# Two triangle layers on one core: quadrants kept in SBUF, LayerNorm roots by Newton's method on VectorE

## The reference, cut to what matters

```
layer 0: z = LN(x);  a = (z@W_ap + b) * sigmoid(z@W_ag + b) * mask;  b likewise
         out[i,j,c] = sum_k a[i,k,c] * b[k,j,c];   x = x + out@W_z + b_z
layer 1: x' = LN(x);  left, right = sigmoid(x'@w1) * (x'@w2)
         p[s,k,e] = sum_r left[s,r,e] * right[k,r,e];  p = LN(p)
         x = x + (p@out_w) * sigmoid(x'@gate)
```

## Time and profile before

| | us |
|---|---|
| median of 3 runs (992.37 to 997.83) | 995.39 |
| the profiled execution's own time | 993.22 |
| its span | 991.6 |
| steps 11 to 47 (VectorE starts of their statistics) | 46.9 to 172.4 |
| contraction 0, first to last matmul | 226.0 to 268.3 |

### The profile page before, as it was taken

How to read it: one execution, slowest core, us unless ns; L and a number is a source line. 1 busy time by engine, 2 the same in 40 slices (tenths; PEclk the granted TensorE clock), 3 DMA queues, 4 the chain that set the end, 5 groups by cost and what they waited for, 6 DMA issues and landing times.

```text
span 991.6 us, 26391 instructions
## 1 busy us (share of the span) xinstructions
PE 817.9 (82%) x9820; PEld 786.3 (79%) x9820; DVE 763.9 (77%) x1851; ACT 635.0 (64%) x866; POOL 590.0 (59%) x410
## 2 busy tenths in 40 slices
PE   4654444567999899989899999999999999999865
PEld 3553344467899799989899999898999898989754
DVE  6899999987589958995388888708980897069896
ACT  5698888765667536753266777547763776257664
POOL 7699999987256504660376444405661667068887
PEclk9789999798999999999899999999999999999999
DMA  4455489988789718969665768857982797876675
GB/s 139 117 161 150 131 275 297 342 286 299 256 274 316 226 33 270 307 205 282 235 194 156 241 214 297 325 193 215 296 279 66 216 306 225 291 253 226 212 233 191
DMA packets 173397, 228.75 MB, mean 231 GB/s; under 512 B 11224, under 2 KB 109784, under 8 KB 171224
## 3 DMA queue, kind: packets, MB, share of 16 engines
q1 hardware_dynamic: 172408, 226.96, 71.7%
q10 hardware_dynamic: 864, 0.12, 0.1%
HBM read 134.76 MB, written 92.27 MB: 229 GB/s over the span
## 4 chain that ended last, share of the span: by engine, by line
PE 43%; DVE 20%; DMA 15%; issue 11%; POOL 4%; ACT 3%; SPq 3%; DVEq 0%; POOLq 0%; ACTq 0%
PE bank L1117 18%; PE ps_w L1151 6%; DVE stats L944 6%; PE bank L1097 6%; DMA xin<-in_x_dram 6%; PE bank L1098 5%; DVE split L988 3%; PE ps_t L1136 3%; DMA xt<-xt 3%; DVE xc L981 2%; DMA xin<-x 2%; PE ps_x L1162 2%; DVE var L951 2%; DVE xc L973 2%; DMA chunk<-xcol 2%
## 5 line engine op out<-in xcount | busy, mean ns | idle before, releaser
L660 POOL TENSOR_TENSOR rstd<-var,minus_half 128x8 f32<-128x8 f32 x192 | 343.8, 1791 | 321.4 <-DVE var L951 321.4
L1117 PE MATMUL bank<-rhs,lhs 128*128 128x128 f32 x1536 | 227.6, 281 | 13.5 <-DVE lhs L924 7.5
L1117 PEld LDWEIGHTS bank<-rhs,lhs 128*128 128x128 f32 x1536 | 200.2, 196 | 16.4 <-DVE lhs L924 8.2
L718 ACT ACTIVATE sig<-bank 128x512 f32<-128x512 f32 x256 | 152.0, 602 | 63.5 <-PE bank L1098 61.1
L745 ACT ACTIVATE xt<-ps_x 128x1024 bf16<-128x1024 bf16 x128 | 130.9, 1022 | 60.6 <-PE ps_x L1162 47.1
L1162 PE MATMUL ps_x<-ident_b,split 128*128 128x128 bf16 x1024 | 83.3, 227 | 95.8 <-DVE split L988 95.3
L1162 PEld LDWEIGHTS ps_x<-ident_b,split 128*128 128x128 bf16 x1024 | 67.1, 102 | 107.3 <-DVE split L988 106.0
L981 DVE TENSOR_TENSOR xc<-xc,rstd 128x504 f32<-128x504 f32 (+1 forms) x192 | 137.9, 718 | 16.1 <-POOL xc L674 13.9
L1097 PE MATMUL bank<-w_rhs,chunk 128*128 128x128 bf16 x1024 | 136.9, 228 | 6.5 <-DVE rhs L916 2.7
L1098 PE MATMUL bank<-w_rhs,chunk 128*128 128x128 bf16 x1024 | 136.0, 227 | 0.0
L1097 PE MATMUL bank<-w_lhs,chunk 128*128 128x128 bf16 x928 | 125.8, 227 | 9.4 <-DVE lhs L916 4.4
(11 more groups left out here) (114 smaller groups left out, 1592.3 us busy)
## 6 DMA issues: line engine op xcount, KB each, us to landing
chunk<-xt SPq DMA_DIRECT2D x90, 512.0 KB, 4.5
xt<-xt SPq DMA_DIRECT2D x80, 512.0 KB, 5.4
xin<-in_x_dram SPq DMA_DIRECT2D x128, 256.0 KB, 4.7
x<-xin SPq DMA_DIRECT2D x64, 256.0 KB, 5.1
xin<-x SPq DMA_DIRECT2D x64, 256.0 KB, 4.9
out_dram<-xin SPq DMA_DIRECT2D x64, 256.0 KB, 4.6
spill<-lhs SPq DMA_DIRECT2D x8, 1024.0 KB, 5.4
chunk<-xcol SPq DMA_DIRECT2D x16, 512.0 KB, 5.6
```

The lines of the kernel that those rows point to most:

```text
L660: g.tensor_tensor(rstd[:, m % 2], var[:, m % 2], minus_half[:, :], ALU.pow).then_inc(rooted, 1)
L718: a.activation(sig[:, s], v[:, 0:C, :], ACT.Sigmoid).then_inc(gated, 1)
L1117: last = mm(bank[:, n], operand_of(q // 4, "lhs", kh)[:, c, :], operand["rhs"][:, kh, c, :], start=kh == 0, stop=kh == HALVES - 1)
```

## The change

- **Roots.** For z steps `variance` and `root` go. VectorE computes the root for a pair of steps (128 × 16 values) in ten small operations, numbered 0 to 9: add eps and scale; an integer operation on the bits that gives a first guess; a step of third order; a Newton step. Each waits on the semaphore of the one before. `root_in_gap()` issues one of them, and is called between the larger operations: between the `bn_stats`, behind `make`, `low`, `normalise`, `mask_unit`. Operation 0 follows the statistics of the odd step at once; 8 and 9 follow those of the next even step together. `stats` has four buffers. Steps 64 and on keep the root on GpSimd.
- **Where operands lie.** From pair 6 (step 12) the intermediate values and the root lie in a bank of PSUM (`newton_p`, in `ps_w`), `guess` and `square` in SBUF; from step 12 the normalised tile of even steps is written to PSUM (`normed_p`, in `ps_t`). Before that all are in SBUF.
- **GpSimd** centres all steps below 128, without waiting for `normalise` of the step before, and takes `low` of odd z steps. Its order in a tick is low, mask, centre. Masks are one a tick from 22 to 69; unit u of contraction 0 waits for its own mask only.
- **Residents.** Columns of quadrant 0 go to the free half of `lhs`, those of quadrant 2 into the memory of `quad`; chunks 16 to 31 (rows of quadrants 0 and 2) are projected from there with a stride. Their 16 loads go, and so do `xt_out` and `store_xt` of those quadrants (32 and 16 issues). Quadrant 2's columns are stored in 8 DMAs of 512 KB in place of 16.
- **Schedule.** All z stages from `norm` on are one tick later. Four "last z" ticks in place of six; the second half takes steps 52 to 55. The spills of `lhs` are spread over contraction 0. `loads` and `loads_diag` are issued in ticks 1 and 3.

```diff
...
-DIRECT = CHUNKS
+DIRECT = 2 * CHUNKS
...
-Z_LAGS = dict(load=-2, stats=0, variance=0, root=0, centre=1, norm=1, high=1, low=2, turn_x=2, xt=3,
-              col=3, store=4, project=3, gates=4, make=5)
+Z_LAGS = dict(load=-2, stats=0, centre=1, norm=2, high=2, low=3, turn_x=3, xt=4,
+              col=4, store=5, project=4, gates=5, make=6)
...
-LATE_Z_LAGS = dict(Z_LAGS, turn_x=3, xt=4, col=4, store=5)
+LATE_Z_LAGS = dict(Z_LAGS, turn_x=4, xt=5, col=5, store=6)
...
-    for m in range(3 * STEPS, Z_LATE - 2):
+    for m in range(3 * STEPS, Z_HALF):
         tick("last z", m)
+    late = dict(zip((1, 3, 4, 6), range(Z_HALF, Z_LATE)))
     for i in range(8):
-        tick("second half", {2: Z_LATE - 2, 5: Z_LATE - 1}.get(i), [48 + 2 * i, 49 + 2 * i], spill=(0, 0, i // 2 - 1) if i in (3, 5, 7) else None)
+        tick("second half", late.get(i), [48 + 2 * i, 49 + 2 * i], spill={6: (0, 0, 0)}.get(i))
     contraction(0, dict(zip((0, 1, 2, 3, 5, 6, 8, 9), range(Z_LATE, 4 * STEPS))),
-                {0: (0, 0, 3), 3: (0, 1, 0), 7: (0, 1, 1), 11: (0, 1, 2), 15: (0, 1, 3)})
+                {2: (0, 0, 1), 4: (0, 1, 0), 6: (0, 0, 2), 8: (0, 1, 1), 10: (0, 0, 3), 12: (0, 1, 2), 15: (0, 1, 3)})
...
-    if MASK_FIRST <= t < MASK_TWO:
-        return [t - MASK_FIRST]
-    if MASK_TWO <= t < MASK_TWO + C // 8:
-        return [2 * C // 4 + 2 * (t - MASK_TWO), 2 * C // 4 + 2 * (t - MASK_TWO) + 1]
-    return []
+    return range(max(0, t - MASK_FIRST), min(POOL_MASKS, t - MASK_FIRST + 1))
...
+def by_rows(m):
+    return step(m)[0] == "x" or step(m)[1] == 1
...
+    if n < DIRECT + 2:
+        return max(stored, TICK_OF[("store", "step", Z_LATE - 1)])
...
-    return m < Z_EARLY or Z_LATE <= m < P_BASE
+    return m < P_BASE
...
+def low_on_pool(m):
+    return m < X_BASE and m % 2 == 1
...
+            return newton_s if 2 * pair < OTHERS_AT + 5 else newton_p
...
+        normed_p = ps_t[:, :, :].rearrange("p n (a c) -> p (n a) c", c=C)
+        def normed_of(m):
+            if OTHERS_AT + 5 <= m < X_BASE and not low_on_pool(m):
+                return normed_p
+            return xc[:, m % 2]
+        def root_of(m):
+            if m < X_BASE:
+                return newton_of(m // 2)[:, 2 + m // 2 % 2, m % 2]
+            return rstd[:, m % 2]
...
+        resident = {0: operand["lhs"][:, 1].rearrange("p c j -> p (c j)").bitcast(BF16),
+                    2: scratch.bitcast(BF16)}
         sig_staged = [sig[:, n].rearrange("p c t -> p (c t)").bitcast(BF16) for n in range(2)]
         SIG_STAGED = Z_LATE
         def col_buffer(m):
-            if m < 2 * STEPS:
+            q, c0 = m // STEPS, step(m)[3]
+            if q in resident:
+                return resident[q][:, P * c0:P * (c0 + COLS)]
+            if m < SIG_STAGED:
                 return chunk[:, (m // 2) % 2, P * COLS * (m % 2):P * COLS * (m % 2 + 1)]
-            if m < SIG_STAGED:
-                return staged[m % 4]
             return sig_staged[m % 2]
...
+            def store_resident(m):
+                _, rh, _, c0 = step(m)
+                sp.wait_ge(col_done, after(m))
+                sp.dma_start(xcol_dram[rh, :, c0 - COLS:c0 + COLS, :],
+                             resident[2][:, P * (c0 - COLS):P * (c0 + COLS)].rearrange("p (j r) -> p j r", r=P)
+                             ).then_inc(resident_stored, 16)
...
+                if t == 1:
+                    for dst, src in loads:
+                        sp.dma_start(dst, src).then_inc(loaded, 16)
...
+                    if m % 2 and by_rows(m):
                         store_xt(m)
-                    if 2 * STEPS <= m < X_BASE:
+                    if m % 2 and m // STEPS == 2:
+                        store_resident(m)
+                    if m // STEPS == 3:
                         store_cols(m)
...
-                pool.wait_ge(normed, after(m - 1))
...
+                    pool.wait_ge(*low_by(m - 2))
...
+            def low(m):
+                h = m % 2
+                pool.wait_ge(high_done, after(m))
+                g.tensor_tensor(split[:, h, :, 1, 1:], xc[:, h, :, 1:], split[:, h, :, 0, 1:],
+                                ALU.subtract).then_inc(low_p, 1)
...
+                for m in due("low", t):
+                    if low_on_pool(m):
+                        low(m)
+                for n in pool_masks_at(t):
+                    mask_operand(n)
...
+                    if by_rows(m):
+                        xt_out(m)
...
-                dve.wait_ge(*centred_by(m - 2))
+                dve.wait_ge(*centred_by(m - 4))
+                if m - 4 < X_BASE:
+                    dve.wait_ge(rooted_z, after(m // 2 - 2))
...
                 for c in range(0, COLS, 2):
+                    if c:
+                        root_in_gap()
...
+            def root(pair, n):
+                count = 9 * pair
+                minus_var, term = (newton_of(pair)[:, i] for i in range(2))
+                result = newton_of(pair)[:, 2 + pair % 2]
+                if n == 0:
+                    dve.wait_ge(rooted_z, after(pair - 1))
+                    dve.wait_ge(stats_done, after(2 * pair + 1))
+                    v.tensor_scalar(minus_var, stats[:, 2 * (pair % 2):2 * (pair % 2) + 2, :, 2],
+                                    C * EPS, NEWTON, ALU.add, ALU.mult).then_inc(newton, 1)
+                if n == 1:
+                    dve.wait_ge(newton, count + 1)
+                    v.tensor_scalar(guess[:, :, :].bitcast(I32), minus_var.bitcast(I32), -0.5, GUESS, ALU.mult, ALU.add
+                                    ).then_inc(newton, 1)
+                if n in (2, 7):
+                    dve.wait_ge(newton, count + n)
+                    v.tensor_tensor(term, minus_var, guess[:, :, :], ALU.mult).then_inc(newton, 1)
+                if n == 3:
+                    dve.wait_ge(newton, count + 3)
+                    v.tensor_tensor(square[:, :, :], term, guess[:, :, :], ALU.mult).then_inc(newton, 1)
+                if n == 4:
+                    dve.wait_ge(newton, count + 4)
+                    v.tensor_tensor(term, term, guess[:, :, :], ALU.mult).then_inc(newton, 1)
+                if n == 5:
+                    dve.wait_ge(newton, count + 5)
+                    v.scalar_tensor_tensor(term, term, -1.25 / NEWTON, square[:, :, :], ALU.add, ALU.mult
+                                           ).then_inc(newton, 1)
+                if n == 6:
+                    dve.wait_ge(newton, count + 6)
+                    v.scalar_tensor_tensor(guess[:, :, :], term, 1.875, guess[:, :, :], ALU.add, ALU.mult
+                                           ).then_inc(newton, 1)
+                if n == 8:
+                    dve.wait_ge(newton, count + 8)
+                    v.scalar_tensor_tensor(term, term, -0.5 / NEWTON, guess[:, :, :], ALU.mult, ALU.mult
+                                           ).then_inc(newton, 1)
+                if n == 9:
+                    dve.wait_ge(newton, count + 9)
+                    dve.wait_ge(normed, after(2 * pair - 3))
+                    v.scalar_tensor_tensor(result, term, 1.5, guess[:, :, :], ALU.add, ALU.mult
+                                           ).then_inc(rooted_z, 1)
+            def root_in_gap():
+                if unfinished:
+                    pair, n = unfinished.pop()
+                    root(pair, n)
+                    if n < 9:
+                        unfinished.append((pair, n + 1))
...
-                v.tensor_tensor(xc[:, h, :, lo:], xc[:, h, :, lo:],
-                                rstd[:, h].unsqueeze(2).broadcast_to([P, COLS, C - lo]),
+                dve.wait_ge(*((rooted, after(m - X_BASE)) if m >= X_BASE else (rooted_z, after(m // 2))))
+                v.tensor_tensor(normed_of(m)[:, :, lo:], xc[:, h, :, lo:],
+                                root_of(m).unsqueeze(2).broadcast_to([P, COLS, C - lo]),
...
+                begun_earlier = [pair for pair, n in unfinished]
+                root_in_gap()
                 for h in halves[:-1]:
                     make(h)
+                    root_in_gap()
                 for m in due("stats", t):
                     statistics(m)
+                    while unfinished:
+                        root_in_gap()
+                    if m < X_BASE and m % 2:
+                        unfinished.append((m // 2, 0))
+                        root_in_gap()
                 for h in halves[-1:]:
                     make(h)
+                    root_in_gap()
                 unit = unit_at(t)
                 if unit and unit[0] in VECTOR_MASKS:
                     mask_unit(*unit)
...
+                for m in due("low", t, "z"):
+                    if not low_on_pool(m):
+                        low(m)
+                        root_in_gap()
+                for m in due("norm", t, "z"):
+                    while unfinished and unfinished[0][0] == m // 2:
+                        root_in_gap()
+                    normalise(m)
+                    root_in_gap()
...
```

(13 more changed lines are left out.)

183 lines of the change are left out of this document (98 added, 85 removed).

## The result

The kernel after takes 1022.1 us (median of four runs, 1017.6 to 1024.8); the kernel before took 996.6 beside it (992.4 to 998.5). The experiments ran in later batches, on different chips, and the kernel before took 993.0 to 996.5 beside them. A difference between two batches is therefore good to some 4 us; the stages of the profiled executions are the finer measure. The ratio is 1.0258, 95% interval 1.0207 to 1.0308. The forecast was 965 (949 to 987): the sign is wrong, and the time is 57 us off.

A forecast was written before the change was run, and what follows sets the result against it. VectorE, with GpSimd close, was taken to bound most of the first 172 us, then DMA, and PE from 226 us. The terms −3 − 3.4 − 9.6 − 15.6 + 1 = −30.6 took 995.4 to 965 us (949 to 987).

The forecast's parts named there:

- Residents: Step 48 to contraction 0: chunk loads and xt stores go, VectorE's gate waits vanish; 53.6 us becomes 38, 15.6 off.
- Start-up: Up to step 11: weight loads move behind later x loads, so step 11 starts 3 us earlier; ends no gain and 3.8.
- the lock: VectorE operations with two SBUF inputs and GpSimd operations exclude each other for a whole instruction; not expected with a PSUM operand.
- Steps 11 to 21: Before the masks start: a step falls from 3.21 to 2.9 us, 3.4 us saved over 11 steps.
- Steps 22 to 47: With masks on GpSimd: a step falls from 3.47 to 3.1 us, 9.6 us saved over 26 steps.
- Second half: Step 48 to the first contraction matmul: four ticks at 3.1 and eight of two chunks at 3.2 each, 15.6 us off.
- Contraction 0: From 226 us: roots leave, GpSimd has a mask in each of ten ticks; 44 us, +1; ends 36 and 52.
- Behind it: After contraction 0: hardly any work changed, spills only delay x loads; no gain or loss in the sum.
- The small operations do not overlap: Rival on the root's operations: each costs 0.22 us, 1.1 a step, VectorE 3.5; 987 us, chance 0.14.
- milder form: Errata rule of fixed cycles per VectorE operation: 0.87 us a step, VectorE 3.25, some 8 us above the forecast.
- The lock holds the small operations: Rival, steps 0 to 51: a PSUM operand does not spare them, 2.25 us a step; +86, about 1080, chance 0.07.
- GpSimd gives it back: Rival: GpSimd's low halves take 1.53 us and contraction 0 takes 52; 12 more, 977 us, chance 0.12.

The follow-up runs named there:

- e15_pitch260: Kernel after with each row of the two resident quadrants beginning 260 bytes behind the last in place of 256, small tiles moved to make room; 976.4 us, ratio 0.9823.
- e7_halves: Kernel after with each resident quadrant stored as two blocks of 64 rows, rows read at 128 bytes, columns loaded as two halves; 979.6 us, ratio 0.9874.
- e5_step260B: Kernel after with chunks 16 to 31 read at a step of 260 bytes, 125 of 128 elements of each vector (wrong vectors); 1033.0 us in one run.
- e6_small_ops_sbuf: Kernel after with chunks 16 to 31 read contiguously (wrong vectors) and all operands of the root's small operations in SBUF; 1077.0 us in one run.

## Why the prediction was wrong

**The step that failed** is "Residents". It removed the loads of chunks 16 to 31 and kept their projections at their old price; that these would now read their stationary operand at 256 bytes in place of 32 stands in the diff and in no term of the sum. The kernel before could have warned: its trace has the same loads at two steps. Contiguous ones took 98 ns (85 to 130 us); the row chunks', at 32 bytes, 149 (142 to 180 us, kernel before):

```profile
L1098 PEld LDWEIGHTS bank<-w_lhs,chunk 128*128 128x128 bf16 x89 | 11.4, 149 | 0.0
```

So the price moved with the step, and the new step lay eight times beyond the last known one: an unknown to be bounded, up to a case in which TensorE decides. That other engines would be held could not be read from that trace. The missing term measured 45.7 us (e15_pitch260 against the kernel after; 43 by the ratios, 44.2 by the stages); 965 + 45.7 = 1010.7, and the other terms miss by the remaining 11 (16 in the profiled execution of e15_pitch260, which lies 2.4 above its median).

**The other terms**, by e15_pitch260:
- *Start-up*, −3 forecast, +2.5 measured. Of a gain of 5.3 the prediction gave 2.3 back to the lock and a tick of latency. The lock alone cost more: two operations of a pair at 1.01 and 1.07, a third at 0.81, 8.3 us before step 11. The move of the weight loads, from which the gain was to come, is worth no more than 0.2.
- *Steps 11 to 21*, −3.4 forecast, −0.2 measured. From step 11 to step 12 it takes 5.05: the last pair in SBUF, held as shown above, which is 2.1 of the 3.2 us missed. The ten steps behind it take 3.02 in the mean, since more long than short ones fall among them; the pace of a pair is 2.92 a step, as forecast (2.9).
- *Steps 22 to 47*, −9.6 forecast, −13.9 measured. VectorE's 2.9 was right, GpSimd's 3.1 too high: its low half takes 1.14 and not 1.28, so that its work is 1.04 + 0.57 + 1.27 = 2.88, and the 0.15 of starting gaps did not come on top. The masks cost no time.
- *Second half*, −15.6 forecast, −8.1 measured (45.5 us, not 38). Ticks of two halves were forecast at 3.2. In e7_halves VectorE waits for gates seven times, 7.4 us (6.9 in e15_pitch260), and nine small operations of a pair stand there back to back, 0.2 each, since there is no large operation left to hide them:

```profile
DVE lhs L999 <- ACT sig L793: 7.4, 7, 2.0
```
- *Contraction 0*, +1 forecast, +2.8 measured.
- *Behind it* nothing was forecast; it took 702 to 713 us in all kernels, which are equal there, the one before among them (709.0).

**The rivals.** "The small operations do not overlap" fell: they put the next large one off by 0.07 to 0.1. Its milder form, 0.87 a step and a pace of 3.25, fell with it: the pace is 2.92. "The lock holds the small operations" did not come about in the kernel after from step 12 on, and its price came out near: forecast at about 1080 us if PSUM did not spare them, measured 1077.0 with the operands in SBUF. That the totals meet is in part luck: the holds measured 2.0 us a step, not 2.25, and the gains beside them were about 20 us, not 31. "GpSimd gives it back" fell. The loss came by none of them, and the 7% for slower were put on a mechanism that the change had avoided by design.

**The lock and the root.** The prediction said that the trace agrees with a lock for a whole instruction. For GpSimd's centrings, low halves and masks it does. For its root it does not, as far as the profile has the root's span right: in the earlier trace rows a normalisation with two inputs in SBUF takes 0.68 inside the 1.94 of a root, and so do all 25 normalisations and 38 low halves that begin inside one between 46 and 172 us.

**Clock.** The low clock did not stretch the operations. The first stretched ones (128.02, 127.70) fall into two microseconds with a clock of 1.00; and at 0.53 in e5_step260B the statistics take 287 ns, at 0.62 and 0.67 in e6_small_ops_sbuf 282. The slow loads of 125 columns also take 0.32 us from the start, at a clock of 1.00 (128 to 129 us in e5_step260B). What the low clock adds inside the 45.7 us was not separated.

## What to carry to other kernels

When a change moves a tile's layout, look for who reads it as a stationary operand and at which step, and price that read like any other added operation, also for the engines beside it. A resident array with rows of 256 bytes that is read across its rows wants a few bytes of padding: here 4 bytes added to 256 were worth 43 to 46 us, and they turned a loss of 2.6% into a gain of 1.8%. A small VectorE operation with two inputs in SBUF beside a GpSimd that is busy with large ones lasted up to six times as long here; with one of them in PSUM it was not held.

## What the runs showed of the hardware

- A weight load with 128 columns at a step of 256 bytes takes 260 ns and starts every 0.122 us, and while a row of them runs, operations of VectorE, ScalarE and GpSimd are held (a normalisation 2.39 in place of 0.68, statistics with one input in SBUF up to 2.07 in place of 0.29, a ScalarE copy 2.45 in place of 1.01, a mask 2.82 in place of 1.27). All of them read or write SBUF; that it is this access which is held is inferred. The Trainium skill (SBUF — State Buffer, SBUF: two separate sides) says that only the shared port pair causes contention and that PE, ACT and VectorE's own pair never wait on anyone; here ScalarE and VectorE's statistics do, and the measurement decides.
- At 240 and 260 bytes the same load takes 147 and 157 ns and holds no one; at 128 bytes it takes 204 and hardly does (statistics 297 ns in place of 286).
- A VectorE operation with two inputs in SBUF that begins within GpSimd's centring, low half or mask ends 0.02 to 0.04 us after it (905 to 1069 ns in place of 166 to 183); with one operand in PSUM it does not wait. Within GpSimd's root it did not wait either (0.68 in 1.94).
- With 125 columns at 256 or 260 bytes a load starts only every 0.213 or 0.225 us and holds no one, but bounds TensorE; contiguous, 125 columns cost next to nothing (0.058).
- In both slow forms the granted clock fell from 1.00 to near 0.5, the 1.2 GHz level, although TensorE was busy for 50.8 of 51 us in one of them; at 128 bytes, with 36.66 of 51, it stayed at 1.00. It fell without slow loads too, to 0.62 in e6_small_ops_sbuf (85 to 127 us, TensorE busy 25.3 of 42). Why was not tried.
